# A hybrid transformer block on one core: two of four rotary products on GpSimd, normalised rows and minus halves on ScalarE, a free bank and repeated transposes

## What is computed

```
x = x + attention_a(layernorm(x))   # softmax attention, 16 heads, 4 key/value heads
x = x + ffn(layernorm(x))           # "feed-forward 0"
x = x + attention_b(layernorm(x))   # linear causal attention, "linear tiles"
x = x + ffn(layernorm(x))           # "feed-forward 1"
```

## Time and profile before

| | us |
|---|---|
| median of 3 runs | 2059.12 |
| lowest and highest | 2056.25, 2059.63 |
| the profiled execution | 2055.61 |
| its span, first to last instruction | 2053.8 |

### The profile page before, as it was taken

How to read it: one execution, slowest core, us unless ns; L and a number is a source line. 1 busy time by engine, 2 the same in 40 slices (tenths; PEclk the granted TensorE clock), 3 DMA queues, 4 the chain that set the end, 5 groups by cost and what they waited for, 6 DMA issues and landing times. The chain is left out here.

```text
span 2053.8 us, 47783 instructions
## 1 busy us (share of the span) xinstructions
PE 1959.6 (95%) x14944; PEld 795.4 (39%) x14944; DVE 1807.0 (88%) x3351; ACT 1490.4 (73%) x2934; POOL 204.7 (10%) x442
## 2 busy tenths in 40 slices
PE   7999999999999999999999999989998899997995
PEld 4323333333333333333333333324433566665432
DVE  7899999999999999999999999975458699997348
ACT  5348888888888888888888888864556565645757
POOL 2310000000000000000000000032013111122012
PEclk9879999999999999999999999999999999999998
DMA  5431221121122112212211211222000000000002
GB/s 161 125 99 48 68 65 44 51 73 51 44 66 65 44 49 72 54 44 66 65 44 49 72 54 44 56 72 108 23 1 2 1 2 2 3 2 1 1 1 83
DMA packets 110303, 101.33 MB, mean 49 GB/s; under 512 B 52288, under 2 KB 91520, under 8 KB 110192
## 3 DMA queue, kind: packets, MB, share of 16 engines
q1 hardware_dynamic: 110192, 99.97, 17.6%
HBM read 78.84 MB, written 20.77 MB: 49 GB/s over the span
## 5 line engine op out<-in xcount | busy, mean ns | idle before, releaser
L1545 DVE TENSOR_REDUCE mx<-ps 128x1 f32<-128x512 f32 x2048 | 1273.8, 683 | 12.6 <-PE ps L688 8.4
L1149 ACT ACTIVATE YT<-ps 128x512 f32<-128x512 f32 x2048 | 1056.7, 602 | 255.3 <-PE ps L742 255.3
L713 PE MATMUL ps<-YT,work 128*32 128x512 f32 x4096 | 546.2, 605 | 0.0
L688 PE MATMUL ps<-work 64*128 64x512 bf16 x2048 | 456.7, 390 | 5.1 <-DVE mx L1545 3.4
L736 PE MATMUL ps<-work 64*128 64x512 bf16 x2048 | 395.0, 378 | 0.1
L742 PE MATMUL ps<-work 34*128 34x512 bf16 x2048 | 394.1, 378 | 0.0
L688 PEld LDWEIGHTS ps<-work 64*128 64x128 bf16 x2048 | 144.6, 93 | 612.5 <-DVE mx L1545 538.8
L736 PEld LDWEIGHTS ps<-work 64*128 64x128 bf16 x2048 | 142.5, 94 | 83.9 <-ACT YT L1149 16.8
L742 PEld LDWEIGHTS ps<-work 34*128 34x128 bf16 x2048 | 100.6, 94 | 78.3 <-issue 1.4
L713 PEld LDWEIGHTS ps<-YT,work 128*32 128x32 f32 x4096 | 80.7, 108 | 120.5 <-ACT YT L1149 113.3
L844 PE MATMUL ps<-work,c_s 128*128 128x512 f32 x192 | 96.3, 625 | 16.5 <-ACT work L1207 11.3
(11 more groups left out here) (185 smaller groups left out, 1795.0 us busy)
## 6 DMA issues: line engine op xcount, KB each, us to landing
work<-k_scr SPq DMA_DIRECT2D x640, 64.0 KB, 2.1
work<-q_scr SPq DMA_DIRECT2D x640, 32.0 KB, 1.7
o_scr<-o_sb SPq DMA_DIRECT2D x32, 256.0 KB, 2.2
X<-in_L_attn_a_x_dram SPq DMA_DIRECT2D x8, 512.0 KB, 7.2
work<-negt SPq DMA_DIRECT2D x256, 1.0 KB
work<-o_scr SPq DMA_DIRECT2D x16, 256.0 KB
work<-inv_scr SPq DMA_DIRECT2D x16, 256.0 KB
out_dram<-X SPq DMA_DIRECT2D x8, 512.0 KB, 2.9
```

The costliest lines, as they stand in the source:

```text
L688: mm(ps[:, bank_of[x], :], qa[rows, p, jp, qt * P:(qt + 1) * P], ka[rows, p, kc_ * CH:(kc_ + 1) * CH], start=True, stop=True).then_inc(a_m ...
L713: m = mm(ps[32 * j:32 * j + 32, 7, :], vst[:, p, t, :], prob(GROUP * t + j), start=t == 0, stop=t == KTILES - 1)
L1149: fn(prob(u), ps[:, S_BANK + u % S_RING, :], ACT.Exp, scale=HD ** -0.5).then_inc(exp_ok, 1)
L1545: dve.tensor_reduce(mx[:, p, at_:at_ + 1], ps[:, bank_of[x], :], AX_X, ALU.max).then_inc(a_max, 1)
```

## The change

- Rotary products: from tile 2 on DVE makes products 0 and 1 (a*cos, b*sin), POOL products 2 and 3 (b*cos, a*sin), after `output_root` in its queue; `rope_sums` waits for l_rtp.
- `normalise` goes from DVE to ACT, as scale*x+shift. POOL makes the shift, with two more operations in `output_root`. ACT runs it between `turned` and the copy of the outputs.
- `turned_minus` of the linear steps goes from DVE to ACT, behind `spread` where both fall in one step. The sign of MINUS_BY is turned (one more POOL operation in `token_parts`).
- Drain: the spreads of chunks 1 and 2 for feed-forward 1 go to DVE (`scaled`, steps 32 and 33); PE turns chunk 1 after `norm_turn` of the last tile and runs the first layer of the first item in two halves in steps 32 and 33; ACT drains chunk 0 in step 32 and chunk 1 in step 33.
- `first_bank_of(1)` is 3, so that item 1's first layer in both stages waits for no bank.
- `repeat(times)`: transposes of the identity into bank 7, which nobody reads, 14 and 8 in both tails and 8 more in tail 0.

```diff
+        def first_bank_of(n):
+            return 3 if n == 1 else first_bank(n)
...
+                def repeat(times):
+                    for t in range(times):
+                        pe.transpose(ps[:, 7, t % 4 * P:(t % 4 + 1) * P], ident[:], ident[:])
...
-                    if ORDER[n][0] < CYCLES - 1:
+                    if ORDER[n][0] < CYCLES - 1 and (k == 0 or n > 0):
                         first(n)
...
                     fourth(LAST - 3)
+                    repeat(14)
                     second(LAST)
...
                     fourth(LAST + 1)
+                    repeat(8)
                     third(LAST + 3)
                     second(LAST + 5)
                     pe.wait_ge(f_d, NCH)
                     pe.wait_ge(f_ga, 6)
                     turn_chunk(2, 0)
                     fourth(LAST + 3)
+                    repeat(8)
                     project_qk(0, 0)
...
+            def first_half(mt):
+                pe.wait_ge(n_y, 2 * (3 * NCH + 1))
+                if mt == 0:
+                    pe.wait_ge(l_r, TILES)
+                else:
+                    pe.wait_ge(l_x, TILES)
+                for kt in range(KT):
+                    m = mm(ps[:, mt, :], c1_s[:, kt, mt * P:(mt + 1) * P], YT[:, kt, ch(0)], start=kt == 0, stop=kt == KT - 1)
+                if mt == KT - 1:
+                    m.then_inc(f_h1, 1)
...
                     turn_chunk(3, 0)
-                    turn_chunk(3, 1)
...
                 if is_tile(n - 2):
                     out_proj(n - 2, p)
+                if n == TILES:
+                    first_half(0)
                 if is_tile(n - 1):
                     norm_turn(n - 1, 1 - p)
+                if n == TILES:
+                    turn_chunk(3, 1)
+                if n == TILES + 1:
+                    first_half(1)
...
+            def turned_minus(k, c):
+                act.wait_ge(f_mx, k * NCH // 2 + c // 2 + 1)
+                wait(act, f_out, k * NCH + c - 1)
+                act.wait_ge(f_v, k * NCH + c)
+                for t in range(4):
+                    m = fn(turned_x[c % 2][:, t, 0:4:3], X[:, 4 * c + t, :].rearrange("p (q n) -> p q n", q=4)[:, 0:4:3], ACT.Identity,
+                           bias=end4[:, c, MINUS_BY, t:t + 1], scale=end4[:, c, MINUS, t:t + 1])
+                m.then_inc(f_v, 1)
...
+            def normalise(n, p):
+                wait(act, l_y, n - 1)
+                act.wait_ge(l_rs, n + 1)
+                fn(o_n[:, p, :], o_r[:, p, :], ACT.Identity, bias=shift[:, p:p + 1], scale=rstd[:, p:p + 1]).then_inc(l_n, 1)
...
                     turned(n + 1, 1 - p)
+                if is_tile(n - 1) and n < TILES:
+                    normalise(n - 1, 1 - p)
...
-                    put_rows(3, 0)
-                    put_rows(3, 1)
+                    normalise(n - 1, 1 - p)
...
-                if n in (TILES - 2, TILES - 1):
-                    spread(3, n - TILES + 2)
-                if n == TILES + 1:
-                    spread(3, 2)
+                if n in MINUS_AT:
+                    turned_minus(0, MINUS_AT[n])
+                if n == TILES - 2:
+                    spread(3, 0)
...
                 dve.wait_ge(l_rt, n + 1)
+                wait(dve, l_rtp, n - 1)
...
-                if n in MINUS_AT:
-                    turned_minus(0, MINUS_AT[n])
+                if n >= TILES:
+                    scaled(3, n - TILES + 1)
...
+            def rope_products(n, p, t):
+                pool.wait_ge(l_silu, n + 1)
+                pool.wait_ge(l_rope, n)
+                for i in (2, 3):
+                    u, v = rope_terms(p, t)[i]
+                    m = pool.tensor_tensor(rt[:, i], u, v, ALU.mult)
+                m.then_inc(l_rtp, 1)
...
-                pool.tensor_tensor(rstd[:, p:p + 1], var_e[:, p:p + 1], mhalf4[:, 0:1], ALU.pow).then_inc(l_rs, 1)
+                pool.tensor_tensor(mean_m[:, p:p + 1], mv[:, p, 0:1], minus4[:, 0:1], ALU.mult)
+                pool.tensor_tensor(rstd[:, p:p + 1], var_e[:, p:p + 1], mhalf4[:, 0:1], ALU.pow).then_inc(l_ro, 1)
+                pool.wait_ge(l_ro, n + 1)
+                pool.tensor_tensor(shift[:, p:p + 1], mean_m[:, p:p + 1], rstd[:, p:p + 1], ALU.mult).then_inc(l_rs, 1)
...
                 output_root(n, n % 2)
+                if is_tile(n + 3):
+                    rope_products(n + 3, 1 - n % 2, (n + 3) % TPB)
```

More of the change, by code:

```diff
@@ L278, in hybrid_block @@
         rstd = sb("rstd", [P, 2])
+        mean_m = sb("mean_m", [P, 2])
+        shift = sb("shift", [P, 2])
         parity = sb("parity", [P, 2])
@@ L294, in hybrid_block @@
             o_res f_csum f_sum f_g f_ga f_cb f_h1 f_a1 f_h2 f_a2 f_h3 f_a3 f_z f_th f_cs f_tw f_up f_out f_as f_d z_st f_pre f_pa f_co f_ze f_c3 f_cm f_mx f_u f_v
-            l_par l_vz l_ys l_qk l_vg l_silu l_v l_gt l_g l_gate l_rt l_rope l_t l_kt l_qt l_qx l_e l_em
-            l_o l_s l_sx l_oe l_ot l_r l_bn l_mv l_ve l_rs l_n l_y l_ye l_w l_x
+            l_par l_vz l_ys l_qk l_vg l_silu l_v l_gt l_g l_gate l_rt l_rtp l_rope l_t l_kt l_qt l_qx l_e l_em
+            l_o l_s l_sx l_oe l_ot l_r l_bn l_mv l_ve l_ro l_rs l_n l_y l_ye l_w l_x
             y_st """.split()
@@ L372, in opened, with halves, rope_terms @@
             return sum(1 for m in range(max(n, 0)) if opened_by(m) is not None)
+        def halves(ap):
+            v = ap.rearrange("p (h a e) -> p h a e", a=2, e=HD // 2)
+            return v[:, :, 0, :], v[:, :, 1, :]
+        def rope_terms(p, t):
+            a, b = halves(qk_a[:, p, :])
+            co = cos_s[:, bass.ds(t, 1), :].broadcast_to((P, 2 * HEADS, HD // 2))
+            si = sin_s[:, bass.ds(t, 1), :].broadcast_to((P, 2 * HEADS, HD // 2))
+            return (a, co), (b, si), (b, co), (a, si)
         def through_tiles(eng, visit):
@@ L1164, in spread @@
                 act.wait_ge(n_t, 2 * (g - 1))
+                if (st, c) == (3, 3):
+                    act.wait_ge(n_xn, g)
                 for t in range(4):
@@ L1197, in first @@
                     for mt in range(KT):
-                        m = fn(h1[:, n % 2, mt, :], ps[:, mt, :] if y == 0 else summed(c)[:, mt, :], ACT.Gelu,
+                        m = fn(h1[:, n % 2, mt, :], ps[:, first_bank_of(n) + mt, :] if y == 0 else summed(c)[:, mt, :], ACT.Gelu,
                                bias=bias[:, D1 + mt:D1 + mt + 1])
@@ L1201, in first @@
                     if y == 0:
-                        act.copy(summed(c), ps[:, 0:KT, :]).then_inc(f_as, 1)
+                        b_ = first_bank_of(n)
+                        act.copy(summed(c), ps[:, b_:b_ + KT, :]).then_inc(f_as, 1)
                 def second(n):
@@ L1461, in scaled @@
                 wait(dve, n_t, 2 * (g - 1))
+                if (st, c) == (3, 1):
+                    dve.wait_ge(n_xn, g)
                 for t in range(4):
@@ L1735, in feed_forward @@
                     joined(k, 7)
-            def halves(ap):
-                v = ap.rearrange("p (h a e) -> p h a e", a=2, e=HD // 2)
-                return v[:, :, 0, :], v[:, :, 1, :]
             def rope_products(n, p, t):
@@ L1744, in rope_products @@
                 wait(dve, l_rope, n)
-                a, b = halves(qk_a[:, p, :])
-                co = cos_s[:, bass.ds(t, 1), :].broadcast_to((P, 2 * HEADS, HD // 2))
-                si = sin_s[:, bass.ds(t, 1), :].broadcast_to((P, 2 * HEADS, HD // 2))
-                for i, (u, v) in enumerate(((a, co), (b, si), (b, co), (a, si))):
+                for i, (u, v) in enumerate(rope_terms(p, t)[0:4 if n < 2 else 2]):
                     m = dve.tensor_tensor(rt[:, i], u, v, ALU.mult)
@@ L1785, in gated @@
                 dve.wait_ge(l_ot, n + 1)
+                wait(dve, l_n, n - 1)
                 dve.scalar_tensor_tensor(out=o_r[:, p, :], in0=gate[:, n % 4, :], scalar=1.0, in1=ps[:, 0, 0:DIM],
@@ L1793, in variance @@
             def variance(n, p):
+                wait(dve, l_rs, n - 1)
                 dve.bn_aggr(mv[:, p, :], stats[:]).then_inc(l_mv, 1)
@@ L1796, in variance @@
                 dve.tensor_scalar(var_e[:, p:p + 1], mv[:, p, 1:2], EPS, None, ALU.add).then_inc(l_ve, 1)
-            def normalise(n, p):
-                wait(dve, l_y, n - 1)
-                dve.wait_ge(l_rs, n + 1)
-                dve.tensor_scalar(o_n[:, p, :], o_r[:, p, :], mv[:, p, 0:1], rstd[:, p:p + 1],
-                                  ALU.subtract, ALU.mult).then_inc(l_n, 1)
             def residual(n):
@@ L1979, in token_parts @@
                 pool.tensor_tensor(turn4[:, own], norm4[:, own], beta, ALU.mult).then_inc(f_pa, 1)
-                pool.wait_ge(f_pa, done // 4 + 1)
+                pool.wait_ge(f_pa, done // 2 + 1)
                 signs = one4[:].rearrange("p (a b) t -> p a b t", a=1).broadcast_to(whole)
@@ L1985, in token_parts @@
                 at0, by = affine4[:, own, 0], affine4[:, own, 1]
+                pool.tensor_tensor(by[:, :, MINUS_BY], shifts[0], minus, ALU.mult).then_inc(f_pa, 1)
```

(6 more changed lines are left out.)

14 lines of the change are left out of this document (8 added, 6 removed).

## The result

The changed kernel takes 2047.16 us in the median (2046.22 to 2048.40) against 2057.90 us for the kernel before in the same session (2056.25 to 2059.63). The ratio is 0.9948, with a 95% interval of 0.9931 to 0.9965: it is faster by 10.7 us.

What follows compares the result with a forecast made beforehand. It took PE and, in many linear steps, VectorE as the bound; 12.5-4.7-6-2.5-0.9=-1.6 us gave 2054.0 us for the profiled execution and 2057.5 us for the median, called no change, with a range of 2048 to 2067 us.

Steps and rivals of the forecast that it cites:

- rivals of a fast or slow product: Linear tiles: GpSimd product pitch 0.40 us, giving 2049 (chance 0.30), or 1.0 us, giving 2070 (chance 0.18).
- fast rival: Linear tiles: GpSimd's product is near its copy, 0.40 us, so sums start as before; -10.1 us, 2049; chance 0.30.
- the prediction's estimate of 0.82: Linear tiles: by the skill's factor of two, VectorE's 0.42 us product would take 0.82 us on GpSimd, the sum 5 us worse.
- n%4=1 is lost by ScalarE: Linear tiles: ScalarE's added work delays the drain to YT, and the next tile's energies wait: +0.8 five times, +4.0 us.
- n%4=3: Linear tiles: VectorE's later sums, less 0.20 us to spare at the mask, cost +0.45 us five times, 2.3 us.
- The collision with the copy: Linear tiles, n%4=2 and 3: GpSimd's copy right behind its products makes VectorE's first sum wait another 0.25 us.
- n%4=2: Linear tiles, steps 6 to 22: nothing hides the later sums on VectorE, +0.65 us five times, 3.3 us.
- Bank: Start of feed-forward 0: with bank 3 the second tile's first layer needs no wait and runs at full clock, -4.7 us.
- Drain: Drain into feed-forward 1: chunk 1's spread leaves the path and half the first layer fills a PE gap, -6 us.
- Tail 0: Tail of feed-forward 0: transposes fill PE's gaps so the projections behind them run at full clock, -2.5 us.
- Feed-forward 1: Its tail: transposes let the projection end 1.5 us earlier, but ScalarE waits only 0.91 us for it, -0.9 us.
- The clock rival: Tails and drain: transposes neither keep nor release the clock, the drain runs at half clock; +4.7 us, 2064; chance 0.12.

Runs made afterwards that it cites:

- a: Changed kernel with all four rotary products of every tile on VectorE again, the rest kept: 2037.53 us, 0.9910 of the kernel before.
- e: Changed kernel with only the minus halves back on VectorE: 2045.32 us, 0.9957 of the kernel before.
- c: Changed kernel with products, normalisation and minus halves all on VectorE as before; drain, bank and transposes kept: 2040.87 us, 0.9924 of the kernel before.
- i: As a, but with the second tile of each feed-forward in bank 0 again: 2041.96 us, 0.9938 of the kernel before.
- d: As a, but without the 52 transposes in the tails of both feed-forwards: 2046.80 us, 0.9955 of the kernel before.
- b: Changed kernel with normalisation and minus halves on VectorE again, two products still on GpSimd: 2042.03 us, 0.9926 of the kernel before.
- f: Changed kernel with the mean's sign and the shift moved from GpSimd to VectorE as one operation behind its products: 2048.26 us, 0.9971 of the kernel before.
- g: Changed kernel with one product instead of two on GpSimd, the first rotary sum ahead of the wait: 2037.72 us, 0.9913 of the kernel before.

## Why the prediction was wrong

- **The frame held.** The tiles lose, the edges of the stages win, and GpSimd's product has the pitch 0.68 (0.69 taken from the earlier trace rows). The rivals of a fast or slow product are both out, although the time, 2047.2, lies near the fast rival's 2049: it came from elsewhere. The Trainium skill (GPSIMD Engine Reference, engine selection) warns of two-input operations on GpSimd as about twice as slow; the pitch of 0.68 against VectorE's 0.34 agrees, the duration of 0.72 us lies under the prediction's estimate of 0.82 (twice 0.42 is 0.84), and a bears the warning out.
- **The step that failed: "n%4=1 is lost by ScalarE", +4.0.** It is +0.9 (five times 0.18), and it comes through VectorE: in step 13 its gated row starts 8.72 us behind L971 instead of 8.54, behind sums that start at 5.01 instead of 4.30. I added the 1.64 us of minus halves and the 0.5 of the normalisation to the times of the earlier trace rows as if ScalarE worked without a break, while the same rows gave its waits for PE, 1.29 and 0.31 us. e shows that the minus halves cost nothing, and the drain to YT stayed at 4.59 us, where I had it 1.15 us later. I also had GpSimd's root of the chunk come too late for the spread: it ended at 1719.1, before the spread's start at 1719.40.
- **The other steps of the tiles.** n%4=3: +2.3 forecast, +0.8. The collision with the copy was charged once more than it is there: in before, the sums of these steps start 4.50 behind L944, because the copy was already in their way, and in after 4.89, with 0.20 to spare: +0.19. n%4=2: +2.6 against 3.3, since the first sum took 0.53 us beside the copy, where I had charged 0.25 on top of 0.42. Steps 2 and 3 gave +1.1 (1.3), steps 24 to 28 +1.7 (1.6). In all 7.0 instead of 12.5, and 5 by the ratios of after and c.
- **The terms outside the tiles are right in sum by luck.** The forecast's are in brackets. Bank: -4.7 in place (i against a; -3.95 in after), of which 1.4 (a) to 2.8 (after) are given back at the wait near 1528, not foreseen; after keeps 1.1 of the 4.7 forecast. Drain: -6.5 (-6). Tail 0: -4.1 (-2.5), -3.1 of it up to the first query/key projection and -1.0 behind it, where less of the way ran at half clock. Feed-forward 1: -2.2 (-0.9). Its tail gave -1.0, as forecast; another -1.6 came where the change did nothing, from a projection that ran 1.95 instead of 2.73 us and the instruction behind it, 1.08 instead of 1.95; its start lost 0.5. Together -14.1 forecast, -14.2 in c, -13.9 in after: the 3.6 us too few of the bank stand against 3.4 too many in the other three.
- **The clock rival** is out for the tails: the transposes hold it (d against a).
- **The sum.** With 7 for 12.5 the forecast would have been -7.1, 2052; the measured median is 2047.2. The 5 us between are 3.5 by which the two profiled executions lie at other places around their medians, and 1.2 by which the median of before, 2059.1 in the runs that the forecast began from, came out as 2057.9 in those of the comparison.

What stays open: why the clock falls behind the 2.9 us wait in one case and not in the other. In feed-forward 0 it went with the bank in twelve kernels of twelve, in feed-forward 1 it did not, and no run shows the cause; each kernel has one profiled execution. That the small operations ahead of the products make the difference between b and after is read from the traces; no run moved them without bringing another delay (f did), and none put GpSimd's products ahead of the root and the shift in its queue.

## What to carry to other kernels

Work put on an idle engine costs what its queue does to the work that waits for it, and that engine's busy share says nothing of this: here two products that take VectorE 0.68 us took GpSimd 1.36, and VectorE stood still for 1.5 us ahead of its sums. The version with the products back on VectorE and all the rest kept has 0.9910 of before, and none of the kernels run here is better beyond its interval. Before charging an engine for added work, take its waits ahead of each step from the timeline and fill them first. Fill TensorE's waits with transposes where its clock falls, and judge this by the time over the whole stretch, because the fall may only move.

## What the hardware showed that I had not expected

- VectorE beside GpSimd's two-input product: 0.96 us for 0.42 (product, b), 0.81 for 0.41 (normalisation, b), 0.68 us for one column (f); GpSimd's own product 0.79 to 0.97 for 0.72 (b, f, g). Overlapped, the pair of engines gained nothing (g equals a).
- One-column GpSimd operations in after: the mean's sign takes 0.19 us in all 28 steps, with VectorE standing still, and the shift 0.33 to 0.46 beside it. The earlier trace rows has 0.37 as the median for four columns. It need not be GpSimd that gets longer: in after that operation took 0.20 us beside VectorE's first sum, and the sum took 0.49 us instead of 0.41.
- Fifty-two transposes that nobody reads are worth 9.3 us (d against a), nearly as much as the whole change (10.7).
- The clock behind one and the same wait of TensorE was full in some kernels and half in others, in feed-forward 1 without regard to the bank.
